# A branch prefetch hint at the head of every loop body

## What is computed

```
x = x + _L0_attn_ref(_layernorm(x), ...)
x = x + _L0_xattn_ref(ctx_1024, _layernorm(x))
x = x + _L0_ffn_ref(_layernorm(x), ...)
x = x + _L1_attn_ref(_layernorm(x), ...)
x = x + _L1_xattn_ref(_layernorm(x), ctx_1024, ctx_1024, Wq, bq, Wk, bk, Wv, bv, Wo, bo)
...
# cross-attention of layers 1, 2 and 3: 16 heads of 8 features, 56 queries, 1500 keys
Q = query @ Wq + bq;  K = key @ Wk + bk;  V = value @ Wv + bv
scores = einsum('bhqd,bhkd->bhqk', Q, K) / scale
out = einsum('bhqk,bhkd->bhqd', softmax(scores), V)
return out.reshape(B, 56, 128) @ Wo + bo
```

## Time and profile before

| | us |
|---|---|
| median of three runs | 4919.73 |
| lowest and highest | 4907.74, 4921.61 |
| the profiled execution's own time | 4914.55 |
| its span, first to last instruction | 4912.5 |
| TensorE busy | 4076.0 (83%) |
| VectorE busy | 3097.2 (63%) |
| ScalarE busy | 2149.6 (44%) |
| GpSimd busy | 1472.0 (30%) |

### The profile page before, as it was taken

One profiled execution on the slowest core, in us unless ns is written; L12 is line 12 of the kernel. 1 busy time (PEld: TensorE's weight loads), 2 busy tenths in 40 slices (PEclk: granted clock), 3 DMA queues, 4 the chain that ended last, 5 costly groups with the idle time before them and its releaser, 6 DMA issues. The chain is left out here.

```text
span 4912.5 us, 124247 instructions
## 1 busy us (share of the span) xinstructions
PE 4076.0 (83%) x49374; PEld 2742.5 (56%) x49374; DVE 3097.2 (63%) x5391; ACT 2149.6 (44%) x2693; POOL 1472.0 (30%) x1222
## 2 busy tenths in 40 slices
PE   7987449999997977599999989856659999996398
PEld 5854126666664456366666653323326666664276
DVE  5632557788774545387777763355657777786643
ACT  2234445555553233355555543333445555554010
POOL 0000035555550000254555520021435555551000
PEclk9989769999998999799999999977879999998599
DMA  3043025455552410155555521000025455551276
GB/s 126 0 156 150 2 70 134 125 131 128 128 129 46 111 34 0 43 141 128 125 125 128 128 56 60 34 4 3 0 68 136 122 127 128 127 132 33 50 189 163
DMA packets 252144, 456.80 MB, mean 93 GB/s; under 512 B 135982, under 2 KB 143662, under 8 KB 251470
## 3 DMA queue, kind: packets, MB, share of 16 engines
q1 hardware_dynamic: 251694, 450.05, 35.2%
HBM read 208.15 MB, written 1.72 MB: 43 GB/s over the span
## 5 line engine op out<-in xcount | busy, mean ns | idle before, releaser
L1171 DVE TENSOR_REDUCE x_bank_top<-ps 112x1 f32<-112x500 f32 x2304 | 1411.8, 670 | 405.5 <-PE ps L1009 395.6
L1113 ACT ACTIVATE x_probs_t<-ps 125x1344 f32<-125x1344 f32 x768 | 991.0, 1290 | 940.7 <-PE ps L1028 940.7
L1156 POOL TENSOR_TENSOR x_key_part<-x_key_whole,x_nothing 128x500 bf16<-128x500 f32 x288 | 358.1, 1243 | 2299.8 <-ACT x_key_whole L1104 2299.8
L1028 PE MATMUL ps<-x_queries,x_keys 128*125 128x112 bf16 x9216 | 700.7, 227 | 70.0 <-issue 58.9
L1028 PEld LDWEIGHTS ps<-x_queries,x_keys 128*125 128x125 bf16 x9216 | 599.8, 139 | 206.2 <-issue 179.0
L1009 PE MATMUL ps<-x_keys,x_queries 96*112 96x500 bf16 x2304 | 662.4, 390 | 46.8 <-DMA x_queries<-x_query_part 37.2
L1040 PE MATMUL ps<-x_probs_t,x_values 125*32 125x112 f32 x18432 | 606.1, 265 | 2.0 <-ACT x_probs_t L1113 2.0
L1040 PEld LDWEIGHTS ps<-x_probs_t,x_values 125*32 125x32 f32 x18432 | 419.6, 110 | 266.3 <-ACT x_probs_t L1113 180.4
L1009 PEld LDWEIGHTS ps<-x_keys,x_queries 96*112 96x112 bf16 x2304 | 283.7, 133 | 341.1 <-DVE x_bank_top L1171 120.7
L988 PE MATMUL ps<-x_ctx_t,x_wk 128*128 128x500 f32 x576 | 336.3, 668 | 60.5 <-ACT x_key_whole L1104 58.1
L1160 POOL TENSOR_TENSOR x_key_part<-x_key_left,x_nothing 128x500 bf16<-128x500 f32 x288 | 360.0, 1250 | 22.6
(11 more groups left out here) (461 smaller groups left out, 5202.1 us busy)
## 6 DMA issues: line engine op xcount, KB each, us to landing
x_keys<-x_key_part SPq DMA_DIRECT2D x1152, 187.5 KB, 3.5
x_ctx_t<-in_ctx_t SPq DMA_DIRECT2D x96, 750.0 KB, 4.5
cm_ctx_n<-in_ctx_n SPq DMA_DIRECT2D x32, 768.0 KB, 5.8
cm_ctx_t<-in_ctx_t SPq DMA_DIRECT2D x32, 750.0 KB, 8.2
x_queries<-x_query_part SPq DMA_DIRECT2D x1152, 14.0 KB, 2.3
e_share<-m_weight_scratch SPq DMA_DIRECT2D x32, 490.0 KB
e_spread_out<-m_slot_scratch SPq DMA_DIRECT2D x32, 490.0 KB
e_share<-m_weight_rows SPq DMA_DIRECT2D x32, 448.0 KB, 5.9
```

Source lines behind the costliest of these rows:

```text
L1028: mm = nc.tensor.matmul(ps[0:KC, TURNED + c // VC, RW * (c % VC):RW * (c % VC) + RW], keys[o % 2][:, p, KC * c:KC * c + KC], queries[o % 2 ...
L1113: nc.scalar.activation(probs_t[p % 2].rearrange("k (n c) r -> k n (c r)", c=VC), ps[0:KC, TURNED:TURNED + VR, 0:VC * RW], ACT.Exp, scale=s ...
L1156: nc.gpsimd.tensor_tensor(part[0][:, cols], key_whole[n][:], nothing[:], ALU.add).then_inc(k_high, 1)
L1171: nc.vector.tensor_reduce(bank_top[0:RW, p, n:n + 1], ps[0:RW, n, 0:KB], AX_X, ALU.max).then_inc(topped, 1)
```

## The change

```diff
@@ -88,6 +88,11 @@
     shape = list(a.shape)
     shape[axis] = n
     return a.to_broadcast(shape)
+
+
+def repeat(nc, engine, start, stop):
+
+    return nc.Fori(start, stop, engines=[engine.engine], hint_back_edge=True)
 
 
 def load_stage(chip, out):
...
@@ -274,7 +279,7 @@
         def all_pairs(engine, one_step):
 
             one_step(0, 0, True, False)
-            with engine.Fori(0, NP_ // 2 - 1) as i:
+            with repeat(nc, engine, 0, NP_ // 2 - 1) as i:
                 one_step(2 * i + 1, 1, True, True)
                 one_step(2 * i + 2, 0, True, True)
             one_step(NP_ - 1, 1, True, True)
...
@@ -897,7 +902,7 @@
 
         for i in (-2, -1, 0):
             one_pass(i, i)
-        with engine.Fori(0, (B - 4) // ROUND) as j:
+        with repeat(nc, engine, 0, (B - 4) // ROUND) as j:
             for o in range(1, ROUND + 1):
                 one_pass(ROUND * j + o, o)
         for i in range(B - 3, B + 1):
...
@@ -2264,7 +2269,7 @@
 
                 for u in range(2):
                     spread_keys(u, u)
-                with pool.Fori(1, NP_ // 2) as i:
+                with repeat(nc, pool, 1, NP_ // 2) as i:
                     for u in range(2):
 
                         pool.wait_ge(s["scores_done"], 2 * i + u - 1)
```

More of the change, by code:

```diff
@@ L465, in all_pairs @@
                 one_pair(n, n)
-            with engine.Fori(0, NP_ // RING - 1) as j:
+            with repeat(nc, engine, 0, NP_ // RING - 1) as j:
                 for o in range(FIRST, FIRST + RING):
@@ L477, in _ @@
         def _(sp):
-            with sp.Fori(0, NP_ // RING - 1) as j:
+            with repeat(nc, sp, 0, NP_ // RING - 1) as j:
                 for r in range(RING):
@@ L531, in _ @@
                 one_pair(n, n, n // RING)
-            with pe.Fori(0, NP_ // RING - 1) as j:
+            with repeat(nc, pe, 0, NP_ // RING - 1) as j:
                 for o in range(FIRST, FIRST + RING):
@@ L658, in _ @@
             pe.wait_ge(global_kept, 3)
-            with pe.Fori(0, CYCLES) as i:
+            with repeat(nc, pe, 0, CYCLES) as i:
                 for c in range(CH):
@@ L683, in _ @@
             nc.scalar.activation(gf[:], ps[:, 6, 0:B], ACT.Sigmoid, bias=gb3[:, 0:1]).then_inc(global_kept, 1)
-            with act.Fori(0, CYCLES) as i:
+            with repeat(nc, act, 0, CYCLES) as i:
                 for n, bias in enumerate((cb1, cb2, cb3)):
@@ L709, in _ @@
                 nc.vector.tensor_tensor(x_of[c], x_of[c], y[c], ALU.add).then_inc(stepped, 1)
-            with dve.Fori(0, CYCLES) as i:
+            with repeat(nc, dve, 0, CYCLES) as i:
                 for c in range(CH):
@@ L1359, in _ @@
         def _(sp):
-            with sp.Fori(0, groups // 2) as i:
+            with repeat(nc, sp, 0, groups // 2) as i:
                 for u in range(2):
@@ L1388, in _ @@
                 nc.tensor.matmul(ps[:, c, 0:CT], zero[:], tokens[c], start=True, stop=False, skip_group_check=True)
-            with pe.Fori(0, groups // 2) as i:
+            with repeat(nc, pe, 0, groups // 2) as i:
                 for n in range(N):
@@ L1399, in _ @@
         def _(act):
-            with act.Fori(0, groups // 2) as i:
+            with repeat(nc, act, 0, groups // 2) as i:
                 for n in range(N):
@@ L1409, in _ @@
                 nc.vector.memset(chip.credit[:, u:u + 1], 0.0).then_inc(used[u], 1)
-            with dve.Fori(0, groups // 2) as i:
+            with repeat(nc, dve, 0, groups // 2) as i:
                 for n in range(N):
@@ L1568, in all_steps @@
         def all_steps(engine, one_step):
-            with engine.Fori(0, PAIRS // 2 - 1) as i:
+            with repeat(nc, engine, 0, PAIRS // 2 - 1) as i:
                 for u in range(2):
@@ L1580, in _ @@
                 sp.dma_start(dst[:], chip.dram[name]).then_inc(consts_landed, 16)
-            with sp.Fori(0, PAIRS // 2) as i:
+            with repeat(nc, sp, 0, PAIRS // 2) as i:
                 for u in range(2):
@@ L1886, in all_passes @@
         def all_passes(engine, one_pass):
-            with engine.Fori(0, NP_ - 1) as i:
+            with repeat(nc, engine, 0, NP_ - 1) as i:
                 one_pass(i, True)
```

## The result

| | us |
|---|---|
| before, median of the four runs beside it | 4919.61 (4907.74 to 4921.61) |
| after, median of four runs | 4875.95 (4869.92 to 4882.04) |
| ratio | 0.9916, 95% interval 0.9896 to 0.9936 |
| forecast | 4833, range 4812 to 4890 |
| profiled execution, before and after | 4914.55, 4882.04 |

The change is faster by 43.7 us where 86.6 were forecast. The time lies inside the range, the forecast itself does not hold. The number fits rival 3 (4875), but by luck: its mechanism is not what happened, as the branches show at once. First the page of the changed kernel, then line L905 (L900 of before, five lines lower), sequencer: ns min/median/max, first and last start.

A forecast was written before the change was run, and what follows sets the result against it. TensorE sets the pace, stalled by instruction fetches at L900's taken back edges. Gain 92.5 - 6 (layer 2) - 2 (hints) = 84.5 us, so 4830 profiled; stated as 4833 for the runs' median, range 4812 to 4890.

The forecast's parts named there:

- rival 3: L900's edges: a hit is not free, each still idles 1.5 us and half the clock falls remain; 4875, chance 0.09.
- What bounds it: TensorE's L900 back edge waits for an instruction fetch; stall and clock fall over 18 edges cost 92.5 us, 5.1 each.
- edges near 24.8: Sign of success in L900: edge passes near 24.8 us in layers 1 and 3.
- the part on layer 2: L900, layer 2: target could come late, as the last fetch starts 1.4 us before the branch; 6 us lost, bounds 0 to 32.8.
- layer 2 stays: Rival on L900's layer 2: the target comes too late, so its edges stay uncured; 4862, chance 0.12.
- The hint's own cost: Hint operations in TensorE's 61 other loop iterations, at 68 ns, much of it ahead of waits; 2 us, from 0 to 13.
- Sum: Whole kernel: gain of 92.5 - 6 - 2 = 84.5 us, from 4914.55 to 4830 on the profiled execution's scale.
- 2 falls: Rival on L900's edges: the hint does nothing and only the hints' cost is left; 4921, chance 0.12.
- 4 falls: Rival on TensorE's small loops: hints make branches wait for needless packets, 3.2 us each, so slower; 5020, chance 0.05.
- The part on the other engines' edges: L900: nothing direct from VectorE's branches; its hint should cover a possible hidden refetch in layer 2, within the 32.8 us bound.

The follow-up runs named there:

- pe_only: Against the changed kernel, the hint stands on TensorE's long cross-attention loop alone, three loops and no other; 4842.18 us, ratio 0.9856.

## Why the prediction was half right

**What bounds it.** Right: the branch waits for its target, 5.1 us an edge, and where the target is there in time the whole of it goes, the clock's part too. The kernel with all heads in slot 50 gained 537.28 - 449.56 = 87.7 of the 92.5 us. A cured edge keeps 0.2 to 0.4 us, so "edges near 24.8" was 0.1 to 0.3 low.

**The step that failed** is the assumption in the part on layer 2, that the target is asked for together with the last packet ahead of the branch, and the reading that followed: layers 1 and 3 safe with 6 us in hand, layer 2 at risk with 1.4. The request does go out at that time, in that packet's stead. But it depends on the slot of the branch in its packet, and the change itself moves the slots: 4 hints ahead of layer 1's branch, 7 ahead of layer 2's, 11 ahead of layer 3's. In layer 2 the packet went from 1.4 us ahead to 2.2 to 3.2 us ahead, enough: 31.0 us gained of its 32.8. In layer 3 the 11 slots took the branch over the boundary: 3.6 us gained of 30.9 (179.19 before). A packet that came 6.2 us ahead was a warning, not a reserve: so early a packet means a branch near its packet's end, where a few more instructions carry it over. The rival "layer 2 stays" had the right mechanism (a target asked for too late) at the wrong layer; its price, 4862, is 14 us under the result, and as near as that only because one layer's excess is like another's; the exits and the rotary stages make up the rest.

**The exits** were taken as free, as the earlier trace rows has them. They cost 8.7 us: the head takes the place of the packet behind, on TensorE at layer 1 and on SyncE behind layer 3. The prediction read in the rows that one thing is fetched ahead of the branch and did not ask what is no longer fetched.

**The hint's own cost**, 2 us: on TensorE itself right in size (31 to 40 ns where 68 were taken, and branches of small loops 1 to 18 ns longer), but the rotary stages took 10.3 us more, which lies inside the 0 to 13 that were given and not in the value chosen. The price of the rows is the operation's; the time of a loop in which TensorE pauses and its clock falls isn't made of it. How much of the 10.3 the hints cause is best told by the kernel that has them in these loops alone: 9.0 us in its profiled execution, 1.0019 in the time.

**Sum.** 84.5 forecast; -27.3 for layer 3's edges, +4.2 and -1.2 for layers 2 and 1, -8.7 for the exits, -8.3 for the rotary stages (10.3, of which 2 were counted), -7.8 for the last mixture and -2.9 not placed give the 32.5 us of the profiled execution (4914.55 to 4882.04). By the medians it is 43.7: the profiled execution of before lies 5.1 us under its median, that of after 6.1 over.

**The rivals.** The hint does act (2 falls); a hit is nearly free (3 falls, though its 4875 is the time to within a microsecond; by its own terms, 92.5 - 44 - 2 off 4919.7, it would be 4873); small loops' branches are 216 to 225 ns in the median, none waits for a packet (4 falls). The part on the other engines' edges holds in layer 2: the second instruction queue had a packet behind each edge and has none there after. It still has them where TensorE alone is hinted, and has none in the kernel that leaves out SyncE's hint, so neither of the two brings them; VectorE, with the next longest body (303), is the likely one, which is not shown. All of it is worth 1.7 us (151.50 - 149.83).

A reading that nothing hangs on: the 610 matmuls and weight loads of L532 in the earlier trace rows are more than one iteration's, since the trace has 601 instructions from branch to branch.

**Better than both:** TensorE's hint alone with its head in slot 50, 0.9842 [0.9826, 0.9857] of before, where the change had 0.9916. Most of that is leaving out the other hints (0.9856 [0.9829, 0.9884] without the slot).

## What to carry to other kernels

A branch prefetch hint is worth having where the back edge waits for a fetch; here that was one loop, nearly all of it on one engine (TensorE 86 to 88 us, the others together under 2). Everywhere else it gained nothing, and in the rotary stages hints cost 0.19%. The kernel with all hints but that loop's was 0.44% slower, but much of that is moved places and a stage that varies by itself. Fix the slot of the body's head so that the branch stands past the middle of its packet (slot 163 of 256 here) and not in its last slots, and the head not in the last ones either, and set the hint before the packet with the branch is entered. When an edit adds instructions ahead of a long loop, count where its branch lands before and after; and when a fetch is moved ahead, ask what it displaces, on each engine and on the path out of the loop. Before a difference of 0.3% between two such programs is given a cause, cut the stages: here one without any hint differed by as much.

## What the hardware showed that was not expected

- A hinted target takes the place of the next packet in order; it is not added to it: 14 packets an iteration instead of 15.
- A branch in the first slots of its packet without a hint is dearer than one further back (4.2 us of idle against 3.0 to 3.8 in the kernel before): the packet behind is fetched first.
- A hint 70 instructions ahead of its branch, inside the branch's packet, leaves the passes as they are without one (27.3 to 30.7 us); 490 ahead it does all (24.8 to 25.0).
- Eight added instructions of some 36 ns each in the code ahead of a loop cost its six edges 26 us (175.56 with eleven hints up to the branch, 149.54 with the three of pe_only).
- With hints on all engines, which take 0.6 us of TensorE's time in all, the rotary stages took 7 to 12 us more than before in five kernels, at a lower granted clock; why is open.
